# Two attention layers interleaved in eight slots per image: other slots for query-key projections and group norm

## The reference

```
# first layer
h = group_norm(x, gn_w, gn_b)                       # 32 groups of 4 channels
q, k, v = split(einsum('oc,bcn->bon', qkv_w, h) + qkv_b)
attn = softmax(einsum('bcn,bcm->bnm', q, k) * C ** -0.5)
x = x + einsum('oc,bcn->bon', proj_w, einsum('bcm,bnm->bcn', v, attn)) + proj_b
# second layer
q, k, v = Wq x + bq, Wk x + bk, Wv x + bv           # 16, 16 and 128 channels
x = gamma * einsum('bcj,bij->bci', v, softmax(einsum('bdi,bdj->bij', q, k))) + x
```

## The kernel before

| k | TensorE | VectorE | ScalarE | GpSimd |
|---|---|---|---|---|
| 0 | query-key product 3 | | its copy | gn_root_out |
| 1 | value product 0 | v_tail | v_head, h_head | h_full, split 3 |
| 2 | value product 1 | v_tail | v_head | h_tail |
| 3 | layer 2 query-key 1, query-key product 0 | qk1_tail | qk1_head, copy | x_bias |
| 4 | layer 2 value 0, query-key product 1 | v1_tail, statistics 0 | v1_head, copy | split 0 |
| 5 | query-key product 2 | statistics 1, bn_aggr | copy | split 1 |
| 6 | layer 2 value 1, norm product 0 | v1_tail, gn_second | v1_head | split 2 |
| 7 | layer 2 query-key 0, norm product 1 | qk1_tail, gn_third | qk1_head | x1_bias |

## Time and profile before

### The profile page before, as it was taken

How to read it: one execution, slowest core, us unless ns; L and a number is a source line. 1 busy time by engine, 2 the same in 40 slices (tenths; PEclk the granted TensorE clock), 3 DMA queues, 4 the chain that set the end, 5 groups by cost and what they waited for, 6 DMA issues and landing times.

```text
span 1681.4 us, 43596 instructions
## 1 busy us (share of the span) xinstructions
PE 1539.8 (92%) x16777; PEld 1147.6 (68%) x16777; DVE 1344.3 (80%) x2547; ACT 1216.3 (72%) x1697; POOL 1249.7 (74%) x1039
## 2 busy tenths in 40 slices
PE   4889999999999999999999999999999999999865
PEld 2557777776777767777677777777767777677654
DVE  2578888888888888888888888888888888888853
ACT  2477777777777777777777777777777777777643
POOL 5997877877788777778777778778777887777500
PEclk9999999999999999999999999999999999999986
DMA  2699999999999999999999999999999999999954
GB/s 58 114 170 197 185 185 203 196 193 191 194 187 187 202 189 189 199 191 193 190 196 194 191 194 184 190 203 194 194 187 195 187 190 202 190 177 190 183 111 93
DMA packets 1081117, 305.20 MB, mean 182 GB/s; under 512 B 1067952, under 2 KB 1068624, under 8 KB 1080912
## 3 DMA queue, kind: packets, MB, share of 16 engines
q1 hardware_dynamic: 1079760, 302.41, 101.7%
q10 hardware_dynamic: 1152, 0.00, 0.0%
HBM read 17.13 MB, written 16.78 MB: 20 GB/s over the span
## 4 chain that ended last, share of the span: by engine, by line
PE 43%; ACT 26%; DVE 16%; issue 12%; POOL 2%; DMA 1%; ACTq 0%; POOLq 0%; DVEq 0%; SPq 0%
DVE nmax L493 9%; ACT scores L403 9%; ACT prob L398 8%; PE mixed L698 7%; PE mixed L700 7%; PE mixed L699 7%; PE scores L659 4%; PE scores L684 4%; PE bank_w L766 4%; ACT k_odd L432 3%; PE scores L661 3%; PE scores L660 3%; PE bank_t L719 3%; ACT v_head L450 2%; PE bank_w L756 2%
## 5 line engine op out<-in xcount | busy, mean ns | idle before, releaser
L698 PE MATMUL mixed<-v_head,pt 128*128 128x129 f16 x4096 | 724.8, 224 | 2.5 <-DMA pt<-rows 2.5
L700 PE MATMUL mixed<-v_head,pt 128*128 128x129 f16 x4096 | 724.5, 221 | 0.0
L699 PE MATMUL mixed<-v_tail,pt 128*128 128x128 f16 x4096 | 724.3, 220 | 0.0
L493 DVE TENSOR_REDUCE nmax<-scores 128x1 f32<-128x1024 f32 x512 | 602.9, 1217 | 64.7 <-PE scores L684 45.2
L306 POOL TENSOR_TENSOR rows<-prob,rows 128x1024 f16<-128x1024 f32 x256 | 545.0, 2129 | 21.4
L403 ACT ACTIVATE scores<-scores,nmax 128x1024 f32<-128x1024 f32 x256 | 278.6, 1088 | 343.1 <-DVE nmax L493 343.1
L301 POOL TENSOR_SCALAR rows<-prob 128x1024 f16<-128x1024 f32 x256 | 267.1, 1043 | 269.0 <-ACT prob L398 265.4
L507 DVE SCALAR_TENSOR_TENSOR rows<-scores,rows 128x1024 f16<-128x1024 f32 x256 | 313.5, 1225 | 153.0 <-ACT rows L410 153.0
L699 PEld LDWEIGHTS mixed<-v_tail,pt 128*128 128x128 f16 x4096 | 408.0, 100 | 2.9 <-issue 0.3
L698 PEld LDWEIGHTS mixed<-v_head,pt 128*128 128x128 f16 x4096 | 400.7, 98 | 5.0 <-DMA pt<-rows 3.9
L700 PEld LDWEIGHTS mixed<-v_head,pt 128*128 128x128 f16 x4096 | 398.8, 97 | 0.0
(11 more groups left out here) (93 smaller groups left out, 1922.8 us busy)
## 6 DMA issues: line engine op xcount, KB each, us to landing
x_raw<-in_x_dram SPq DMA_DIRECT2D x32, 512.0 KB, 4.7
out_dram<-y SPq DMA_DIRECT2D x64, 256.0 KB, 2.9
pt<-rows SPq DMA_TRANSPOSE x512, 4.7
w_qkv<-in_L_conv_qkv_w_dram SPq DMA_DIRECT2D x3, 64.0 KB, 3.9
w_proj<-in_L_conv_proj_w_dram SPq DMA_DIRECT2D x1, 64.0 KB, 3.8
w_v<-in_L_conv_Wv_dram SPq DMA_DIRECT2D x1, 64.0 KB, 3.6
b_qk<-in_L_conv_bk_dram SPq DMA_DIRECT2D x4, 0.1 KB, 2.2
b_qk<-in_L_conv_bq_dram SPq DMA_DIRECT2D x2, 0.1 KB, 3.0
```

Source lines behind the costliest of these rows:

```text
L493: nc.vector.reduce_max(nmax[layer][:, t:t + 1], scores[layer][:, :], AX.X, negate=True).then_inc(maxed[layer], 1)
L698: mm(mixed[l][:, 0:C + 1], head, vh[:, im.p, m, 0:C + 1], start=(m == 0), stop=False)
L699: mm(mixed[l][:, 0:C], head, vt[:, im.p, m, :], start=False, stop=False)
L700: done = mm(mixed[l][:, 0:C + 1], tail, vh[:, im.p, m, 0:C + 1], start=False, stop=(m == TILES - 1))
```

## The change

The constants and the literal offsets of the group norm and of the first layer's query-key steps change. Query-key products 0 and 1 go from k = 3, 4 to k = 1, 2 (offsets -5, -4 to -7, -6), and their splits on GpSimd with them, to k = 2, 3. The statistics go from k = 4, 5 to k = 1, 2, the norm products with `gn_second` and `gn_third` from k = 6, 7 to k = 3, 4, `gn_root_out` from k = 0 to k = 5, `h_full` and `h_head_out` from k = 1 to k = 6, `h_tail_out` from k = 2 to k = 7, `x_bias` from k = 3 to k = 4, `x1_bias` from k = 7 to k = 5. The norm products now lie between query-key products 1 and 2 of the image before, so the wait for `gn_dve` moves from product 3 to product 2, and `gn_product` waits for one copy-out fewer.

```diff
--- before.py
+++ after.py
@@ -35,8 +35,9 @@
 SWING = (1, 13)
 ATTEND = (3, 16)
 ADD = (4, 17)
-QK_AT = (-5, -4, -3, 0)
-GN_AT = (-10, -9)
+QK_AT = (-7, -6, -3, 0)
+SPLIT_AT = (-6, -5, -2, 1)
+GN_AT = (-13, -12)
 V_AT = (1, 2)
 QK1_AT = (7, 11)
 V1_AT = (12, 14)
@@ -367,17 +368,17 @@
 
             def body(it):
                 for k in range(8):
-                    if im := at(it, k, -8):
+                    if im := at(it, k, -11):
                         gn_root_out(im)
-                    if im := at(it, k, -7):
+                    if im := at(it, k, -10):
                         h_full(im)
-                    if im := at(it, k, -6):
+                    if im := at(it, k, -9):
                         h_tail_out(im)
-                    if im := at(it, k, 15):
+                    if im := at(it, k, 13):
                         x1_bias(im)
-                    if im := at(it, k, -5):
+                    if im := at(it, k, -4):
                         x_bias(im)
-                    for j, offset in enumerate((-4, -3, -2, 1)):
+                    for j, offset in enumerate(SPLIT_AT):
                         if im := at(it, k, offset):
                             qk_split(im, j)
                     if tile := tile_at(it, k, EXP[0]):
@@ -640,7 +641,7 @@
                             qk1_tail_out(im, h)
                         if im := at(it, k, V1_AT[h]):
                             v1_tail_out(im, h)
-                        if im := at(it, k, -12 + h):
+                        if im := at(it, k, -15 + h):
                             gn_first(im, h)
                     if im := at(it, k, GN_AT[0]):
                         gn_second(im)
@@ -723,11 +724,10 @@
                 if j == 0:
                     pe.wait_ge(h_tail_done, im.n + 1)
                     pe.wait_ge(h_head_done, im.n + 1)
-                if j == 3:
-                    if im.before(-1).exists():
-                        pe.wait_ge(gn_dve, im.n * GN_STEPS + 2 * GN_STEPS)
-                elif j or im.at_least(1):
+                if j or im.at_least(1):
                     pe.wait_ge(qk_out, im.n * 4 + j)
+                if j == 2 and im.before(-1).exists():
+                    pe.wait_ge(gn_dve, im.n * GN_STEPS + 2 * GN_STEPS)
                 cols = slice(h * HALF, (h + 1) * HALF)
                 split_product(bank_t[:, :], w_head[:, s, :], w_tail[:, s, :],
                               h_head[:, im.p, cols], h_tail[:, im.p, cols]).then_inc(qk_made, 1)
@@ -770,7 +770,7 @@
             def gn_product(im, step):
                 if step == 0:
                     if im.at_least(1):
-                        pe.wait_ge(qk_out, im.n * 4 - 1)
+                        pe.wait_ge(qk_out, im.n * 4 - 2)
                     else:
                         pe.wait_ge(consts_made, 7)
                     pe.wait_ge(gn_dve, im.n * GN_STEPS + 3)
```

## The result

| | us |
|---|---|
| median of 4 runs after (1710.54 to 1713.18) | 1711.57 |
| median of 4 runs before | 1681.37 |
| ratio | 1.0179, 95% interval 1.0162 to 1.0197 |
| the profiled execution after, and its span | 1710.54, 1708.8 |

What follows compares the result with a forecast made beforehand. No single engine bounds it: each of an image's eight slots is limited by TensorE's queue or a three-engine ring. Slots summed to 50.35 against 49.43, +25.8 over 28 images, ends -1.8: median 1705.6, range 1692 to 1717.

Steps and rivals of the forecast that it cites:

- c: N minus the next slot's start, carried from slot to slot; into k = 3 forecast at +0.07, about -0.66 before.
- Statistics, the costly part: On VectorE at k = 1 and 2, behind the value tail: N at 6.08 in k = 2, c = +0.07.
- gn_second at k = 3: VectorE does it after two query-key tails, holding back TensorE's transposes; its three instructions add 0.44, slot 7.54 us.
- N: Start of the second layer's row maximum; VectorE work between the reciprocals and the next one lengthens the ring.
- k = 7 and k = 0: k = 7 keeps only the second layer's query-key product: 6.19, loses 0.51; k = 0 gives back 0.38, 6.43.
- h_head at k = 6: 1.25 us on ScalarE ahead of the two norms, which end the slot; length 6.32.
- rival C: h_head hides, alone, with norms not late at k = 6: -0.42 us an image, 1694; chance 8%.
- GpSimd and the load: k = 6 most crowded, row's head 0.4 late without cost; x load still about 11 us ahead; both taken as 0.
- Rival D: More waits: bn_aggr's 0.35 lateness becomes the rule, GpSimd's 0.4 is felt; +0.35 to +0.75 an image, 1715 to 1727; 12%.
- The ends: Start -2 (bounds -5 and 0), first k = 3 +0.7, short k = 7 -0.2, drain -0.3; together about -1.8.
- The clock: Rival: TensorE's standstill at k = 3 drops its clock; up to 2.73 us an image, up to 76, 1780; 3%.
- the ring: Three-engine loop: second layer's row maximum, first layer's, exponentials, next score product, next N; at least 5.8 to 5.9 us.

## Why the prediction was right

- *Direction and size.* Slower, inside the range, 30.2 measured for 24 forecast. The cut into slots and the one number c carried between them gave seven of the eight lengths to 0.02 us. Of the 6.2 us that were missing, 3.4 are 28 images of 0.12 more than forecast, and 2.8 are scatter of the runs: the profiled execution before lies 1.78 above the median of its runs, the one after 1.03 below, so the medians grew by 30.2 and the spans by 27.4.
- *Statistics, the costly part.* c into k = 3 is +0.07 as worked out. Moved elsewhere they free 0.54 an image; one more costs 0.58.
- *gn_second at k = 3: the term that was too small.* The forecast took 0.44 for its three steps, from k = 6 before, and the slot as 7.54; it is 7.64. The three steps before, between the v_tail and the N of the earlier trace rows:

```profile
894.40 0.15 DVE L545 COPY gs<-bank_t 128x1 f32<-128x1 f32 x1
894.47 0.14 DVE L546 TENSOR_TENSOR gs<-mv,bank_t 128x1 f32<-128x1 f32 x1
894.64 0.27 DVE L548 TENSOR_SCALAR gs<-gs,mv 128x1 f32<-128x1 f32 x1
```

  Before, the copy starts 0.08 ahead of v_tail's end (894.48), and the second step 0.07 behind the copy's start. At k = 3 after, the copy starts 0.03 behind the tail's end (892.29), and the second step 0.19 behind the copy's start. From the copy's start to N it is 0.57 instead of 0.44; the copy itself stands 6.66 into the slot where the forecast had 6.69, which leaves the 0.10. 28 times 0.10 is 2.8 us. The 0.19 goes with what stands ahead of the copy: in the five kernels that have gn_second behind the second query-key tail (the changed one, the two extra bn_stats, the statistics elsewhere, h_head behind the norms) it is 0.19 in 29 of 32 images, and in the other eight, with v_tail or the reciprocals ahead, it is 0.06 to 0.08 in all. So the place of gn_second within its slot cost this too. In the program that tail reads from partition 64 on and the steps behind it from partition 0 on; no run varies that alone, so the reason stays open.
- *k = 7 and k = 0.* One wins 0.51, the other gives 0.38 back, to the hundredth. The drain's bare slots were a sound price for slots that the steady part didn't yet have.
- *h_head at k = 6.* Right at 6.33, and the run with it behind the norms shows that only its place ahead of them cost anything. The forecast's rival C had its effect right, -0.42 against -0.45 measured, but for a case that the program's order excludes.
- *Query-key products.* Their cost was forecast as TensorE's length, 6.00 at k = 1 and 2, and paid back at k = 3 and 4; the run with that move alone and h_head behind the norms puts the net at 0.08, with h_head's leaving k = 1 in it.
- *GpSimd and the load, taken at 0.* No steady slot waits for either. At k = 6 GpSimd is busy 6.16 of 6.33 us, and nothing pays.
- *Rival D, the late bn_aggr.* It comes again in one image of 28, at 1491.79 behind 0.50 of idling, and the k = 3 of that image is 7.99 long, 0.35 more than the others. Its price was right, and it didn't become the rule.
- *The ends: the sum right by luck, both parts wrong.* -1.8 was forecast and -1.7 measured: the span grew by 27.4 and the 28 images by 29.1. The start was to win 1.5 and wins nothing: the first of the 28 images, from its k = 3 on, begins at 128.8 before and 128.7 after. The first product does come 3.8 earlier, at 16.51 instead of 20.30, but the first score product stands at 28.95, where it was 29.18. Most of this is lost between the second query-key product, at 18.92, and the third: the norm products of image 1 now lie between them, and the third comes 4.53 behind the second, where it was 2.30 (22.61 to 24.91):

```profile
22.55 0.56 PE L781 MATMUL bank_t<-gs,group_mean 128*128 128x1 f32 x2 [0.81 <-DVE gs L549]
23.45 0.59 PE L660 MATMUL bank_t<-h_head,w_head 128*128 128x512 f16 x1 [0.34 <-DVE gs L554]
```

  Another 1.16 goes to h_full of image 1, which GpSimd now does ahead of the third split, for which the first score product waits:

```profile
25.79 1.19 POOL L331 TENSOR_SCALAR h<-x_raw,gs 128x1024 f32<-128x1024 f32 x1 [0.22 <-ACT qk L425]
26.95 0.62 POOL L363 TENSOR_SCALAR qk_head<-qk 128x512 f16<-128x512 f32 x1
27.66 1.15 POOL L366 TENSOR_TENSOR qk_tail<-qk,qk_head 128x512 f16<-128x512 f32 x1
```

  In the first images, where a slot holds one layer, GpSimd from 34.47 to 80 goes from one instruction to the next without a pause, and its h_full and split at k = 6 and its h_tail at k = 7 are felt in ScalarE's wait for a row tail:

```profile
73.44 1.11 ACT L399 ACTIVATE prob<-scores,ebias 128x1024 f32<-128x1024 f32 x1 [3.36 <-POOL rows L307]
```

  Before, the same exponential, at 73.83, waits 2.10, and for VectorE. So the cover that I named for GpSimd (three slots to the row's use) isn't there while the pipeline fills. The drain is 1.6 us shorter, of which the forecast had 0.3: its k = 3 and 4 are 6.19 and 6.51 long instead of 6.77 and 6.27. From its k = 5 on the changed kernel and the one with the norm steps ahead of the tails have the same program, and yet it took 153.8 us in the profiled execution of the one and 155.1 in that of the other; before it was 155.1. So the other 1.3 is scatter and no gain of the change.
- *The clock.* The granted clock is 1.00 in k = 3, though TensorE stands still for 0.93 us ahead of its transposes. The forecast took the Trainium skill's rule on gaps (TensorE: Matmul & The Clock Gate, "HAM oscillation — how this bites in real kernels") for a rival with 3%; no trace here shows it in the steady part, even with k = 3 at 8.22. That section tells of an array that waits for DMA between its blocks of products, so it spoke less plainly against this change than the forecast put it.

What stays open: why the second step of gn_second stands 0.12 us farther behind the first at k = 3, and what the query-key products cost for themselves beside the value products.

## What to carry to other kernels

In a schedule written out slot by slot, carry the lateness of the ring from slot to slot beside each slot's length: a step is priced by whether its engine idles at that point of its own queue, and the same bn_stats cost 0.58 or nothing. What a slot wins is partly given back by the next one (0.94 and 0.59; 0.51 and 0.38), so a wait that the profile names is more than its removal alone won here. Before a step is moved to another slot, look at its place within the slot: small steps that another engine waits for go ahead of long ones that wait themselves, and steps that nobody waits for behind those that hold the others.

## What the runs showed of the hardware that was not expected

Two one-column instructions of VectorE that don't depend on each other (a copy, then a subtraction) start 0.07 us apart at k = 6 of the kernel before and 0.19 apart at k = 3 after, 892.32 and 892.51. The same holds in every run by what stands ahead of them: 0.19 behind the second query-key tail, 0.06 to 0.08 behind v_tail or the reciprocals. Nothing else was unexpected; in the kernel after, the length of a slot repeats to 0.02 us over the 28 images but for one k = 3 (7.99) and one k = 4 (6.33).
